# Cross attention blocks with the maximum steps in groups of three and four

## The chip, the cores and the metric

The kernel runs on one core of a Trainium2 chip. The metric is the device time of one execution in microseconds. TensorE does the matmuls and transposes (PE, with its weight loads as PEld), VectorE is DVE, ScalarE is ACT, GpSimd is POOL, and SyncE (SP) issues most DMAs. Each engine takes its own instructions strictly in program order, and semaphores order the engines among each other.

## The reference, cut to what matters

Two post-norm decoder layers on x of shape (4, 1024, 256). Each layer is `x = layernorm(x + self_attention(x))`, `x = layernorm(x + cross_attention(x, ctx))`, `x = layernorm(x + ffn(x))`. The change touches the two cross attentions alone (16 heads of 16, 77 context tokens, a padding mask in the first layer only):

```
Q = x @ Wq + bq ; K = ctx @ Wk + bk ; V = ctx @ Wv + bv     # 16 heads of 16
attn = softmax(Q K^T / 4, over the 77 keys, masked in layer 0)
y = layernorm(x + (attn @ V) @ Wo + bo)
```

## The kernel before, in words

`cross_attention` is called twice, once for each layer (tiles c_...). Its 4096 tokens go in NB = 8 blocks of 512. X, the residual stream, lies in SBUF throughout. One function, `walk`, is run for every engine: it writes down all steps in one order, and each engine takes from each step its own instructions. So the order of the calls in `walk` and `block_of` is the order of work of each engine, POOL's too, and no engine passes a waiting instruction.

The steps of a block n are these.

- `turn_x` (L1006, two halves): PE transposes X, ACT copies it to xT.
- `queries` (L1025, four column groups c): two f32 matmuls, recorded as four; ACT copies to qF with bias and scale; POOL casts to qR.
- `largest` (L1046, sixteen times, c and token tile tt): one matmul of queries with keys into a bank, then a DVE maximum (L1059) that frees the bank.
- `turn_max` (L1064): PE transposes the maxima, ACT copies them to nT, SP writes them by four DMAs into spare rows of qF, so that the later scores come out with the maximum subtracted.
- `scores` (L1084, four times): PE, then ACT's exponential (L1104 with the mask, L1106 without) over psS. There is one psS, so the next scores wait for the exponential.
- `values` (L1109, four times): PE multiplies by V and a column of ones into psO; DVE transposes psO to tok (L1123), takes a reciprocal (L1125), multiplies into oC (L1127), and at every second c transposes oC to oT (L1131).
- `add_bias` (L1138, two halves): POOL makes xb = X + bo.
- `outputs` (L1148, two halves): PE multiplies oT by wo; DVE adds xb to give res (L1166), then computes the moments (bn_stats, bn_aggr, L1169 to L1173); POOL works out the scale and shift in four small operations (rstd, L1182 to L1185).
- `normed` (L1190): ACT writes the normalized rows back to X.

`turn_x`, `queries`, `largest`, `turn_max` and `outputs` share the three PSUM banks of psM in rotation:

```
def bank(w):
    return w.count.get("mi", 0) % RB
```

A step that takes a bank waits until the step three places earlier in that rotation has been read out by DVE or ACT. The blocks are pipelined: during block n the kernel does the maxima of block n+1, the queries of block n+2, and the outputs of block n-1. In the second layer a helper (`hall`, called by `also` and `choice_step`) spreads the token choice of the next stage over blocks 3 to 7: on DVE `weigh` (two operations) and `count` (one operation over 1024 values), on POOL eight indirect DMAs in block 7.

Of the kernel before, what the change touches and what calls it, by code (L numbers as in the profile page):

```python
# [859 lines left out]
def cross_attention(nc, tag, X, y, kv, w_q, b_q, w_k, b_k, w_v, b_v, w_o, b_o, mask, hall=None):  # L860

    B, TK, _ = kv.shape
    NT = X.shape[1]
    H, HD, R, NQ = 16, 16, 32, 4
    BT = 512
    NB = NT * P // BT
# [7 lines left out]
    with ExitStack() as ctx:  # L875
        m = Room(nc, ctx, tag)
# [27 lines left out]
        res = m.sb("res", [P, 2, 2, D])  # L904
# [12 lines left out]
        sems = {n: m.sem(n) for n in names}  # L917
        block = ctx.enter_context(nc.Block())

        came = {}  # L920
# [33 lines left out]
        def keys(w):  # L954
            if w.on("tensor"):
                w.wait("wk", NS)
                for cc in range(2):
                    w.wait(*came["cx", cc])
                for c in range(NQ):
                    for cc in range(2):  # L960
                        last = w.eng.matmul(psS[:, c, 0:B * TK], wk[:, cc, c * P:(c + 1) * P], cxT[:, cc, :],
                                            start=cc == 0, stop=cc == 1)
                    last.then_inc(sems["k"], 1)
            w.inc("k", NQ)
            if w.on("scalar"):
                for c in range(NQ):
                    w.wait("k", c + 1)
                    w.eng.activation(kF[:, c, :], psS[:, c, 0:B * TK], ACT.Identity, bias=bks[:, c:c + 1])\
                        .then_inc(sems["kf"], 1)
            w.inc("kf", NQ)  # L970
            if w.on("vector"):
                for c in range(NQ):
                    w.wait("kf", c + 1)
                    for i in range(4):
                        rows = slice(R * i, R * i + R)
                        kf = kF[rows, c, :].rearrange("p (b k) -> p b k", b=B)
                        if mask is not None:
                            last = w.eng.scalar_tensor_tensor(kblk[rows, c, :, i, :], mbias[rows, :, :], sel17[rows, :], kf,
                                                              ALU.mult, ALU.add)
                        else:  # L980
                            last = w.eng.tensor_copy(kblk[rows, c, :, i, :], kf)
                        last.then_inc(sems["kb"], 1)
            w.inc("kb", 4 * NQ)
# [125 lines left out]
        def values(w, n, c):  # L1109
            b = n // BB  # L1110
            seq = w.count.get("pv", 0)
            if w.on("tensor"):
                if seq < 2:
                    w.wait(*came["v", seq])
                w.wait("ex", seq + 1)
                w.wait("tk", w.at("tk"))
                for i in range(4):
                    last = w.eng.matmul(psO[R * i:R * i + R, :], vP[:, b, 4 * c + i, :], E[:, seq % 2, i, :], start=True, stop=True)
                last.then_inc(sems["pv"], 1)
            w.inc("pv")  # L1120
            if w.on("vector"):
                w.wait("pv", w.at("pv"))
                w.eng.transpose(tok[:, :], psO[:, :]).then_inc(sems["tk"], 1)  # L1123
                w.wait("tk", w.at("tk", -1))
                w.link(w.eng.reciprocal(inv[:, :], tok[:, HD::R]), "dv")  # L1125
                half = c % 2
                w.link(w.eng.tensor_tensor(oC[:, :].rearrange("p (g r) -> p g r", r=R)[:, :, half * HD:(half + 1) * HD],  # L1127
                                           tok[:, :].rearrange("p (g r) -> p g r", r=R)[:, :, 0:HD],
                                           inv[:, :].unsqueeze(2).to_broadcast([P, BT // R, HD]), ALU.mult), "dv")
                if half:  # L1130
                    w.eng.transpose(oT[:, n % 2, c // 2, :], oC[:, :]).then_inc(sems["ot"], 1)  # L1131
            else:
                w.inc("dv", 2)
            w.inc("tk")
            if c % 2:
                w.inc("ot")

        def add_bias(w, n, half):  # L1138
# [9 lines left out]
        def outputs(w, n, half):  # L1148
# [13 lines left out]
            if w.on("vector"):  # L1162
                w.wait("mi", w.at("mi"))
                w.wait("xb", w.at("xb"))
                w.wait("y", w.at("y"))
                w.eng.tensor_tensor(res[:, half, :, :].rearrange("p a c -> p (a c)"), psM[:, k, :],  # L1166
                                    xb[:, half, :, :].rearrange("p a c -> p (a c)"), ALU.add).then_inc(sems[f"m{k}"], 1)
                w.wait(f"m{k}", w.at(f"m{k}", -1))
                w.eng.bn_stats(bst[:, half, 0, :], res[:, half, 0, :])  # L1169
                w.link(w.eng.bn_stats(bst[:, half, 1, :], res[:, half, 1, :]), "dv")  # L1170
                w.eng.memset(idle[:, :], 0.0)
                w.eng.bn_aggr(mv[:, half, 0, :], bst[:, half, 0, :])
                w.eng.bn_aggr(mv[:, half, 1, :], bst[:, half, 1, :]).then_inc(sems["var"], 1)  # L1173
            else:
                w.inc("dv")
            w.inc(f"m{k}")
            w.inc("var")
            if w.on("gpsimd"):
                if n or half:
# [64 lines left out]
        def block_of(w, n):  # L1244

            def big(*cs):
                if n + 1 < NB:
                    for c, tt in cs:  # L1250
                        largest(w, n + 1, c, tt)

            def ask(c):
                if n + 2 < NB:
                    queries(w, n + 2, c)

            def turn(half):
                if n + 2 < NB:
                    turn_x(w, n + 2, half)

            def put(half):
                if n:
                    outputs(w, n - 1, half)

            def norm(half):
                if n:
                    normed(w, n - 1, half)

            def also(c):
                if hall is not None:  # L1270
                    choice_step(w, n, c)

            big((0, 0))
            put(0)
            big((0, 1))
            turn(0)
            big((0, 2))
            scores(w, n, 1)
            big((0, 3))
            turn(1)  # L1280
            big((1, 0), (1, 1))
            also(0)
            values(w, n, 0)
            norm(0)
            ask(0)
            big((1, 2), (1, 3), (2, 0))
            scores(w, n, 2)
            add_bias(w, n, 0)
            big((2, 1), (2, 2))
            ask(1)  # L1290
            also(1)
            values(w, n, 1)
            big((2, 3), (3, 0))
            put(1)
            big((3, 1), (3, 2))
            scores(w, n, 3)
            big((3, 3))
            also(2)
            values(w, n, 2)
            if n + 1 < NB:  # L1300
                turn_max(w, n + 1)
            norm(1)
            add_bias(w, n, 1)
            ask(2)
            ask(3)
            also(3)
            values(w, n, 3)
            if n + 1 < NB:
                scores(w, n + 1, 0)

        def walk(w):
            for cc in range(2):
                turn_context(w, cc)
            keys(w)
            for half in range(2):
                turn_x(w, 0, half)
            for c in range(NQ):
                queries(w, 0, c)
            for half in range(2):
                turn_x(w, 1, half)  # L1320
            if mask is not None:
                turn_mask(w)
            for c in range(NQ):
                for tt in range(4):
                    largest(w, 0, c, tt)
                    if c < 2 and tt == 1:
                        context_values(w, c)
                queries(w, 1, c)
            turn_max(w, 0)
            scores(w, 0, 0)  # L1330
            for n in range(NB):
                block_of(w, n)
            if hall is not None:
                rank(w, 1)
                hall.load(w, 0)
            for half in range(2):
                outputs(w, NB - 1, half)
            for half in range(2):
                normed(w, NB - 1, half)
            if hall is not None:  # L1340
                for t in range(2):
                    hall.scatter(w, 1, t)
# [50 lines left out]
        def _(eng):  # L1393
# [5 lines left out]
            eng.dma_start(wo[:, :, :], w_o.rearrange("(a p) o -> p a o", p=P)).then_inc(sems["wo"], 16)  # L1399
            eng.dma_start(bo[:, :], b_o.partition_broadcast(P)).then_inc(sems["wo"], 16)  # L1400
            eng.preload_act_table(ACT.Exp)
            eng.wait_ge(sems["cstv"], 8)
            walk(Writer(nc, eng, "scalar", sems))

        @block.tensor
        def _(eng):
            eng.wait_ge(sems["cst"], 6)
            eng.wait_ge(sems["cstv"], 8)
            walk(Writer(nc, eng, "tensor", sems))

# [1382 lines left out]
```

## Time and profile before

| | |
|---|---|
| median of 3 runs | 3086.0 us (3080.34 to 3092.77) |
| profiled execution | 3086.83 us, span 3085.1 us |
| granted TensorE clock, mean | 0.94 |
| busy shares of the span | PE 87%, PEld 52%, DVE 55%, ACT 38%, POOL 51% |
| first cross attention | about 1787 to 2059 us of the span |
| second cross attention | about 2646 to 2930 us of the span |

A line of the timeline gives the start, the duration, the engine, the source line, the operation and its tiles, how many instructions were merged, and in brackets how long the engine was idle before it and what released it. Matmuls overlap, so the cost of a step on PE is read from its start to the next step's start.

### The profile page before, as it was taken

The page shows a single profiled execution, that of the slowest core. Times are in us where ns is not written, and L with a number is a line of the kernel's source. Part 1 is how long each engine was busy: PE and PEld are TensorE (multiplying, and loading weights), DVE is VectorE, ACT ScalarE, POOL GpSimd, SP SyncE. Part 2 cuts the span into 40 slices and gives each one's busy share as a digit, 9 for nine tenths or more (in the row PEclk, how much of TensorE's full clock was granted, in tenths as well). Part 3 has the DMA queues.
Part 4 walks back from the last instruction along what each step waited for, and adds up shares of the span by engine and source line. Part 5 has one row for each costly group of instructions (what it writes and reads, how often), then busy time and mean ns, then how long its engine had stood idle before and what let it go on. Part 6 is the DMA issues. An engine that isn't in the chain of part 4 may idle for free. (4 is left out here: it accounts for less than half of the span.)

```text
span 3085.1 us, 40725 instructions
## 1 busy us (share of the span) xinstructions
PE 2689.0 (87%) x11441; PEld 1611.1 (52%) x11441; DVE 1682.7 (55%) x3323; ACT 1176.0 (38%) x1638; POOL 1560.1 (51%) x1298
## 2 busy tenths in 40 slices
PE   7999999999999999999999868971786498588696
PEld 5666666666666666666665433340554244334254
DVE  5665656565565666656566435651223555368753
ACT  3444444444443444444343324540122244244334
POOL 2666667766666776666677712225223312222343
PEclk9999999999999999999999989985998599799798
DMA  4333333323333333333323120024773100000143
GB/s 123 77 78 74 78 80 74 71 70 80 72 80 80 71 72 73 80 70 82 80 70 79 38 85 2 2 69 162 268 266 134 50 1 0 29 2 8 30 136 89
DMA packets 142457, 238.07 MB, mean 77 GB/s; under 512 B 27638, under 2 KB 72990, under 8 KB 137246
## 3 DMA queue, kind: packets, MB, share of 16 engines
q1 hardware_dynamic: 126510, 166.81, 21.7%
q0 software_dynamic: 11904, 64.06, 6.1%
q10 hardware_dynamic: 3952, 6.08, 0.6%
q8 instruction: 47, 0.77, 0.1%
q14 instruction: 44, 0.36, 0.0%
HBM read 89.52 MB, written 29.38 MB: 39 GB/s over the span
## 5 line engine op out<-in xcount | busy, mean ns | idle before, releaser
L636 POOL TENSOR_TENSOR a_total<-a_total,a_pr 128x1024 f32<-128x1024 f32 x384 | 910.6, 2371 | 70.5 <-ACT a_pr L620 50.3
L567 DVE TENSOR_REDUCE a_nmax<-a_psX 128x1 f32<-128x512 f32 x1024 | 694.2, 688 | 150.7 <-PE a_psX L562 148.3
L620 ACT ACTIVATE a_pr<-a_psS 128x1024 f32<-128x1024 f32 x512 | 524.8, 1026 | 656.0 <-PE a_psS L608 650.9
L648 PE MATMUL a_psO<-a_pr,a_vd 128*64 128x512 f32 x2048 | 481.8, 602 | 0.0
L562 PE MATMUL a_psX<-a_kA,a_qA 128*128 128x512 f32 x1024 | 414.7, 406 | 7.7 <-DMA a_kA<-a_klo 4.5
L636 POOL TENSOR_TENSOR a_total<-a_pr 128x1024 f32<-128x1024 f32 x64 | 152.9, 2388 | 516.8 <-ACT a_pr L620 516.8
L608 PE MATMUL a_psS<-a_qA,a_kA 128*128 128x512 f32 x1024 | 347.9, 421 | 1.6 <-DVE a_nT L583 1.4
L608 PE MATMUL a_psS<-a_qB,a_kB 128*128 128x512 f32 x1024 | 322.3, 396 | 1.9 <-DVE a_qB L591 1.9
L648 PEld LDWEIGHTS a_psO<-a_pr,a_vd 128*64 128x64 f32 x2048 | 130.0, 136 | 248.3 <-issue 212.1
L608 PEld LDWEIGHTS a_psS<-a_qA,a_kA 128*128 128x128 f32 x1024 | 184.8, 190 | 124.0 <-issue 90.0
L562 PEld LDWEIGHTS a_psX<-a_kA,a_qA 128*128 128x128 f32 x1024 | 193.8, 189 | 89.9 <-DVE a_nmax L567 15.2
L608 PEld LDWEIGHTS a_psS<-a_qB,a_kB 128*128 128x128 f32 x1024 | 193.6, 189 | 40.6 <-DVE a_qB L591 3.0
L1043 POOL CAST c_qR<-c_qF 128x512 fp32r<-128x512 f32 x64 | 39.2, 613 | 218.4 <-ACT c_qF L1038 218.4
L1059 DVE TENSOR_REDUCE c_nmx<-c_psM 128x4 f32<-128x308 f32 x256 | 110.3, 467 | 64.0 <-PE c_psM L1054 62.6
L582 DVE COPY a_nT<-a_psX 8x128 f32<-8x128 f32 x64 | 17.8, 279 | 222.8 <-PE a_psX L577 222.8
L1033 PE MATMUL c_psM<-c_xT,c_wq 128*128 128x512 f32 x256 | 121.1, 608 | 8.0 <-ACT c_xT L1020 5.3
L1054 PE MATMUL c_psM<-c_kblk,c_qR 128*128 128x308 f32 x256 | 92.8, 404 | 28.3 <-DVE c_nmx L1059 14.3
L480 DVE STREAM_TRANSPOSE a_turned<-a_psM 128x512 f32<-128x512 f32 x64 | 45.9, 717 | 124.7 <-PE a_psM L430 124.7
L2483 ACT ACTIVATE e_hT<-e_psH,e_wt 128x128 f32<-128x128 f32 x160 | 45.6, 368 | 177.8 <-PE e_psH L2475 177.8
L658 ACT ACTIVATE a_oU<-a_psO 128x512 f32<-128x512 f32 x64 | 38.2, 597 | 184.1 <-PE a_psO L648 180.1
L1054 PEld LDWEIGHTS c_psM<-c_kblk,c_qR 128*128 128x128 f32 x256 | 46.3, 192 | 115.3 <-issue 95.6
L2442 PE MATMUL e_psT<-e_ident,e_xg 128*128 128x128 f32 x80 | 19.4, 328 | 93.8 <-DMA e_xg<-sorted_in 93.8
(366 smaller groups left out, 4215.2 us busy)
## 6 DMA issues: line engine op xcount, KB each, us to landing
a_qA<-a_qhi SPq DMA_DIRECT2D x256, 128.0 KB, 2.3
a_kA<-a_khi SPq DMA_DIRECT2D x128, 128.0 KB, 2.3
a_kA<-a_klo SPq DMA_DIRECT2D x128, 128.0 KB, 2.3
a_kB<-a_khi SPq DMA_DIRECT2D x128, 128.0 KB, 2.3
a_qB<-a_qlo SPq DMA_DIRECT2D x128, 128.0 KB, 2.3
a_vd<-a_vg SPq DMA_DIRECT2D x128, 128.0 KB, 2.3
sorted_in<-g_zero SPq DMA_DIRECT2D x4, 1280.0 KB, 11.3
e_xg<-sorted_in SPq DMA_DIRECT2D x40, 128.0 KB, 4.3
```

The source lines that it names most:

```text
L480: w.eng.transpose(turned[:, :], ps[:, :]).then_inc(sems["md"], 1)
L562: w.eng.matmul(psX[:, half, :], qA[:, b, u * P:(u + 1) * P], kA[:, b, half * 512:(half + 1) * 512], start=True, stop=True).then_inc(sems[" ...
L567: w.eng.tensor_reduce(nmax[:, half, u:u + 1], psX[:, half, :], AX.X, ALU.max, negate=True)\
L608: last = w.eng.matmul(psS[:, half, q, :], kt[:, b, kc * P:(kc + 1) * P], qt[:, b, q * 512:(q + 1) * 512], start=a == 0, stop=a == 1)
L620: w.eng.activation(pr[:, n, :], psS[:, half, :, :].rearrange("p a b -> p (a b)"), ACT.Exp, scale=SCALE)\
L636: w.eng.tensor_tensor(total[:, buf, :], first, pr[:, n, :], ALU.add).then_inc(sems["ad"], 1)
L648: last = w.eng.matmul(psO[q * HD:(q + 1) * HD, :], vd[:, b, kc, :], pr[:, n, q * 512:(q + 1) * 512], start=kc == 0, stop=kc == KC - 1)
L1033: last = w.eng.matmul(psM[:, k, :], wq[:, cc, c * P:(c + 1) * P], xT[:, cc, :], start=cc == 0, stop=cc == 1)
L1043: w.eng.tensor_copy(qR[:, n % 2, c, :], qF[:, n % 3, c, :]).then_inc(sems["qr"], 1)
L1054: w.eng.matmul(psM[:, k, 0:K4], qR[:, n % 2, c, tt * P:(tt + 1) * P], kblk[:, c, b, :, :].rearrange("p i k -> p (i k)"), start=True, stop= ...
L1059: w.eng.tensor_reduce(nmx[:, tt, 4 * c:4 * c + 4], psM[:, k, 0:K4].rearrange("p (i k) -> p i k", k=TK), AX.X, ALU.max, negate=True).then_i ...
L2483: last = w.eng.activation(hT[:, par, a, :], psH[:, par, a, :], GELU, bias=wt[:, slot, B1 + a:B1 + a + 1])
```

## The change

The same operations are issued as before, in another order. In `values` the reciprocal, the multiplication and the transpose to oT become a step of their own, `divided`; in `outputs` the moments (DVE) and the scale and shift (POOL) become a step `moments`. `add_bias` is now called right ahead of `outputs` of the same half. The order within a block is rewritten, with the maximum steps in groups of three, three, three, three and four. `turn_x` goes three blocks ahead. In the front of `walk`, two of the four query steps of block 1 stand ahead of the first scores and two behind it, and PE and ACT no longer wait at their start for DVE's constants. Of `block_of` the diff below shows the new order alone; the old one is at L1273 to L1309 above.

```diff
@@ keys
             if w.on("scalar"):
+                w.eng.wait_ge(sems["cstv"], 8)
@@ values
                 w.wait("pv", w.at("pv"))
+                w.wait("dv", w.at("dv"))
                 w.eng.transpose(tok[:, :], psO[:, :]).then_inc(sems["tk"], 1)
-                w.wait("tk", w.at("tk", -1))
+            w.inc("tk")
+
+        def divided(w, n, c):
+            half = c % 2
+            if w.on("vector"):
+                w.wait("tk", w.at("tk"))
                 w.link(w.eng.reciprocal(inv[:, :], tok[:, HD::R]), "dv")
@@ outputs
                                     xb[:, half, :, :].rearrange("p a c -> p (a c)"), ALU.add).then_inc(sems[f"m{k}"], 1)
-                w.wait(f"m{k}", w.at(f"m{k}", -1))
+            w.inc(f"m{k}")
+            came["res", half] = (f"m{k}", w.at(f"m{k}"))
+
+        def moments(w, n, half):
+            if w.on("vector"):
+                w.wait(*came["res", half])
                 w.eng.bn_stats(bst[:, half, 0, :], res[:, half, 0, :])
@@ block_of (the new order; largest is called by big)
             def put(half):
                 if n:
+                    add_bias(w, n - 1, half)
                     outputs(w, n - 1, half)
+
+            def shape(half):
+                if n:
+                    moments(w, n - 1, half)
+            big(3)
+            if n:
+                divided(w, n - 1, 3)
+            ask(0)
+            scores(w, n, 1)
+            big(3)
+            values(w, n, 0)
             put(0)
+            divided(w, n, 0)
+            scores(w, n, 2)
+            big(3)
+            shape(0)
             also(0)
+            values(w, n, 1)
+            put(1)
+            divided(w, n, 1)
             norm(0)
+            big(3)
+            scores(w, n, 3)
+            big(4)
+            shape(1)
+            also(1)
+            values(w, n, 2)
             ask(1)
             if n + 1 < NB:
                 turn_max(w, n + 1)
             norm(1)
+            divided(w, n, 2)
+            also(2)
             ask(2)
             ask(3)
+            if n + 3 < NB:
+                turn_x(w, n + 3, 0)
+                turn_x(w, n + 3, 1)
+            values(w, n, 3)
             also(3)
             if n + 1 < NB:
                 scores(w, n + 1, 0)
@@ walk
+            turn_max(w, 0)
+            for c in range(2):
                 queries(w, 1, c)
-            turn_max(w, 0)
             scores(w, 0, 0)
+            for c in range(2, NQ):
+                queries(w, 1, c)
+            for half in range(2):
+                turn_x(w, 2, half)
             for n in range(NB):
                 block_of(w, n)
+            divided(w, NB - 1, 3)
             for half in range(2):
+                add_bias(w, NB - 1, half)
                 outputs(w, NB - 1, half)
+                moments(w, NB - 1, half)
@@ tensor
-            eng.wait_ge(sems["cst"], 6)
-            eng.wait_ge(sems["cstv"], 8)
+            eng.wait_ge(sems["cst"], 2)
```

## Rows read from the trace of the kernel before

**Rows 1.** Windows: busy PE, PEld, DVE, ACT, POOL; clock, DMA; blocks 1-5 and rest, both attentions.

```profile
1866.87:2005.59 138.72, 123.95 (x624) 56.02 (x621) 86.78 (x210) 70.57 (x75) 37.49 (x71) 1.00 0.01 2
2005.59:2059.40 53.81, 37.75 (x200) 17.36 (x196) 33.72 (x84) 22.51 (x21) 13.27 (x29) 0.90 0.01 1
...
2719.80:2858.60 138.80, 124.59 (x624) 56.12 (x620) 102.78 (x238) 69.17 (x75) 38.17 (x71) 1.00 0.02 6
2858.60:2930.00 71.40, 45.22 (x218) 20.97 (x214) 55.88 (x138) 21.68 (x21) 22.89 (x39) 0.76 0.17 32
```

**Rows 2.** Timeline of PE, first score step of blocks 0, 1 and 7, and of block 0.

```profile
1837.42 2.00 PE L1093 MATMUL c_psS<-c_qF,c_kF 32*77 32x512 f32 x8 [4.41 <-DMA c_qF<-c_nT]
...
1866.87 1.10 PE L1093 MATMUL c_psS<-c_qF,c_kF 32*77 32x512 f32 x8
...
2028.61 2.00 PE L1093 MATMUL c_psS<-c_qF,c_kF 32*77 32x512 f32 x8 [2.63 <-DMA c_qF<-c_nT]
...
2693.80 2.01 PE L1093 MATMUL c_psS<-c_qF,c_kF 32*77 32x512 f32 x8 [4.35 <-DMA c_qF<-c_nT]
```

**Rows 3.** Timeline of PE inside block 2 of the first cross attention.

```profile
1907.28 1.10 PE L1093 MATMUL c_psS<-c_qF,c_kF 32*77 32x512 f32 x8
1908.30 0.55 PE L1054 MATMUL c_psM<-c_kblk,c_qR 128*128 128x308 f32 x2
1908.69 1.88 PE L1033 MATMUL c_psM<-c_xT,c_wq 128*128 128x512 f32 x4
1910.50 1.07 PE L1118 MATMUL c_psO<-c_E,c_vP 77*32 77x512 f32 x8
...
1911.88 1.89 PE L1158 MATMUL c_psM<-c_wo,c_oT 128*128 128x256 f32 x8
```

**Rows 4.** Timeline of ACT and DVE inside blocks 2 and 3.

```profile
1899.14 0.69 DVE L1166 TENSOR_TENSOR c_res<-c_psM,c_xb 128x512 f32<-128x512 f32 x1 [1.72 <-PE c_psM L1158]
...
1900.82 0.83 DVE L1059 TENSOR_REDUCE c_nmx<-c_psM 128x4 f32<-128x308 f32 x2
...
1908.44 1.96 ACT L1104 ACTIVATE c_E<-c_psS,c_mb 77x2048 f32<-77x2048 f32 x1 [1.62 <-PE c_psS L1093]
...
1916.18 1.22 DVE L1059 TENSOR_REDUCE c_nmx<-c_psM 128x4 f32<-128x308 f32 x3
...
1923.33 0.25 DVE L1125 RECIPROCAL c_inv<-c_tok 128x16 f32<-128x16 f32 x1
...
1924.08 0.71 DVE L1131 STREAM_TRANSPOSE c_oT<-c_oC 128x512 f32<-128x512 f32 x1
1924.72 0.44 DVE L1059 TENSOR_REDUCE c_nmx<-c_psM 128x4 f32<-128x308 f32 x1
```

**Rows 5.** Timeline, end of the second layer's self attention.

```profile
2637.58 0.15 DVE L2218 BATCH_NORM_AGGREGATE s_mv<-s_bst 128x2 f32<-128x6 f32 x1
...
2639.35 1.26 POOL L2191 TENSOR_TENSOR s_xb<-X,s_bo 128x512 f32<-128x512 f32 x1
...
2640.71 0.69 DVE L2211 TENSOR_TENSOR s_res<-s_psX,s_xb 128x512 f32<-128x512 f32 x1 [2.98 <-issue]
```

**Rows 6.** PE's wait in block 0, first and second cross attention; windows behind the first.

```profile
1855.96 0.38 PE L1054 MATMUL c_psM<-c_kblk,c_qR 128*128 128x308 f32 x1 [2.55 <-DVE c_nmx L1059]
...
2712.16 0.38 PE L1054 MATMUL c_psM<-c_kblk,c_qR 128*128 128x308 f32 x1 [2.55 <-DVE c_nmx L1059]
...
1858.00:1864.00 6.00, 6.00 (x17) 2.16 (x10) 1.66 (x4) 1.98 (x2) 0.00 (x0) 0.50 0.02 4
```

**Rows 7.** Timeline, front of the first cross attention.

```profile
1795.24 0.32 DVE L1380 TENSOR_SCALAR c_mbias<-c_mraw 128x308 f32<-128x308 uint8 x1 [5.49 <-DMA c_mraw<-mask]
...
1797.88 6.88 PE L961 MATMUL c_psS<-c_cxT,c_wk 128*128 128x308 f32 x16 [0.61 <-ACT c_cxT L936]
...
1815.03 0.87 PE L1054 MATMUL c_psM<-c_kblk,c_qR 128*128 128x308 f32 x2
...
1832.40 0.60 PE L1070 MATMUL c_psM<-c_ident,c_nmx 128*16 128x128 f32 x4
```

More of the change, by code:

```diff
@@ L1122, in values @@
                 w.wait("pv", w.at("pv"))
+                w.wait("dv", w.at("dv"))
                 w.eng.transpose(tok[:, :], psO[:, :]).then_inc(sems["tk"], 1)
-                w.wait("tk", w.at("tk", -1))
+            w.inc("tk")
[3 more added lines that the diff above has]
+                w.wait("tk", w.at("tk"))
                 w.link(w.eng.reciprocal(inv[:, :], tok[:, HD::R]), "dv")
-                half = c % 2
                 w.link(w.eng.tensor_tensor(oC[:, :].rearrange("p (g r) -> p g r", r=R)[:, :, half * HD:(half + 1) * HD],
@@ L1133, in values @@
                 w.inc("dv", 2)
-            w.inc("tk")
-            if c % 2:
+            if half:
                 w.inc("ot")
@@ L1175, in outputs @@
                 w.inc("dv")
-            w.inc(f"m{k}")
             w.inc("var")
@@ L1244, in block_of, with big @@
         def block_of(w, n):
-            def big(*cs):
-                if n + 1 < NB:
-                    for c, tt in cs:
+            steps = [(c, tt) for c in range(NQ) for tt in range(4)]
+            def big(count):
+                for _ in range(count):
+                    c, tt = steps.pop(0)
+                    if n + 1 < NB:
                         largest(w, n + 1, c, tt)
@@ L1255, in ask @@
                     queries(w, n + 2, c)
-            def turn(half):
-                if n + 2 < NB:
-                    turn_x(w, n + 2, half)
             def put(half):
                 if n:
+                    add_bias(w, n - 1, half)
                     outputs(w, n - 1, half)
+            def shape(half):
+                if n:
+                    moments(w, n - 1, half)
             def norm(half):
@@ L1271, in also @@
                     choice_step(w, n, c)
-            big((0, 0))
-            put(0)
[L1275 to L1281, printed above, removed]
+            big(3)
[5 more added lines that the diff above has]
+            values(w, n, 0)
+            put(0)
+            divided(w, n, 0)
+            scores(w, n, 2)
+            big(3)
+            shape(0)
             also(0)
-            values(w, n, 0)
+            values(w, n, 1)
+            put(1)
+            divided(w, n, 1)
             norm(0)
[L1285 to L1289, printed above, removed]
-            ask(1)
[L1291 to L1299, printed above, removed]
+            big(3)
[4 more added lines that the diff above has]
+            values(w, n, 2)
+            ask(1)
             if n + 1 < NB:
@@ L1302, in block_of @@
             norm(1)
-            add_bias(w, n, 1)
+            divided(w, n, 2)
+            also(2)
             ask(2)
             ask(3)
+            if n + 3 < NB:
+                turn_x(w, n + 3, 0)
+                turn_x(w, n + 3, 1)
+            values(w, n, 3)
             also(3)
-            values(w, n, 3)
             if n + 1 < NB:
@@ L1318, in walk @@
                 queries(w, 0, c)
[L1319 to L1322, printed above, removed]
             for c in range(NQ):
@@ L1325, in walk @@
                     largest(w, 0, c, tt)
-                    if c < 2 and tt == 1:
-                        context_values(w, c)
+                    if tt == 1:
+                        if c < 2:
+                            turn_x(w, 1, c)
+                        else:
+                            context_values(w, c - 2)
+                if c == 0 and mask is not None:
+                    turn_mask(w)
+            turn_max(w, 0)
+            for c in range(2):
                 queries(w, 1, c)
-            turn_max(w, 0)
             scores(w, 0, 0)
+            for c in range(2, NQ):
+                queries(w, 1, c)
+            for half in range(2):
+                turn_x(w, 2, half)
             for n in range(NB):
                 block_of(w, n)
+            divided(w, NB - 1, 3)
             if hall is not None:
@@ L1406, in _ @@
         def _(eng):
-            eng.wait_ge(sems["cst"], 6)
-            eng.wait_ge(sems["cstv"], 8)
+            eng.wait_ge(sems["cst"], 2)
             walk(Writer(nc, eng, "tensor", sems))
```

## Prediction

> **What bounds the kernel now.** I read three views: the windows of each cross attention, to see which engine fills them; PE's timeline over one block, to see where PE stands still; and the other engines' timelines, for what releases it. Only the cross attentions are touched, 272 and 284 us of 3085. In blocks 1 to 5 PE is busy 124 of 138.7 us at full clock, DVE 87 (103 in the second attention, which has the token choice), ACT 71 and POOL 37 [rows 1]. So PE's in-order stream sets the pace, with its waits. Five blocks take 138.7 us, 27.74 each. In the second attention blocks 6, 7 and the tail (71.4 us) are another case: PE is busy 45, DVE 56.
>
> **The durations.** PE, start to next start [rows 3]: scores 1.02; two maximum steps 0.39, three about 0.5; queries 1.81 with their tail, 1.72 back to back (estimate from four records); values 1.38 less a pair's 0.39, so 0.99; outputs about 1.7 of the 1.89 recorded. The work of a block is 4 x 1.02 + 16 x 0.15 + 4 x 1.72 + 4 x 0.99 + 2 x 1.7 + about 1.1 of transposes = 21.9 us, which leaves 5.8 us of waits and tails per block to be won. DVE [rows 4]: a maximum 0.41; adding xb 0.70 and the moments 0.98 (together 1.68); reciprocal and multiply 0.75, with the transpose to oT 1.39. Transposing psO to tok takes about 0.75 and starts 1.2 behind values. An exponential starts 1.16 behind its scores and lasts 1.96. DVE starts to add about 2.0 behind the start of outputs, and ACT starts to read a query bank about 1.95 behind its start (estimates: the step's own length plus the lag of 0.3 that scores show).
>
> **The new block, walked.** Let t = 0 be the start of the first scores, with everything at full clock. Maxima 1.0; queries wait for the first bank until 2.0; scores 3.7; maxima 4.8; values 5.3; outputs (first half) 6.3 to 8.0; scores 8.0; maxima 9.0; values 9.5; outputs (second half) 10.5 to 12.2. DVE adds the first half at 8.2, divides to 9.7, does three maxima to 10.9, and the moments end at 12.0. This is where the change bites itself. POOL's order is now: bias of half 0, scale and shift of half 0 (it waits for the moments), bias of half 1. DVE's next addition needs that second bias. What this costs is not shown in the cross attention of before, where both biases are made a half block ahead. But the self attention of the second layer has the same order at its end: the moments end at 2637.73, POOL's bias starts at 2639.35 and DVE's addition at 2640.71, 2.98 us later [rows 5]. So the second addition starts at 15.0 and ends at 15.7. The third maximum behind outputs takes the bank of outputs, so PE stands from 12.5 to 15.8: **one gap of 3.3 us in every block**. Queued behind it are the fourth scores, and on DVE the second division and seven maxima.
>
> From there: scores 15.9; DVE divides to 17.1, then takes seven maxima with four PE steps waiting for three banks, until 19.9; values 19.0; queries 19.9; turn_max 21.7; queries 22.1 and 23.8; two turns of x 25.5; values 26.2; next scores **27.3**. The maxima reach qF in time: in before, turn_max at 1832.40 is followed by the scores at 1837.42 [rows 2, 7], 5.0 us, here 26.7. So the new order, which without POOL's order would make a block of about 24.9 (the second addition at 12.7 in place of 15.0, PE's gap 0.9), makes one of 27.3, 0.4 under 27.74.
>
> **The clock.** The price of the gap is larger than its length. In block 0 of before both attentions have the same wait of 2.55 us [rows 6]. In the first one the clock then fell to 0.50 from 1858 to 1864 and the block took 1866.87 - 1837.42 = 29.45; in the second it held and the block took 2719.80 - 2693.80 = 26.00 [rows 1, 2]. So a fall at this place costs 3.45. After the waits of 2.63, 4.35 and 4.41 the scores ran 2.0 us in place of 1.1: half clock every time [rows 2]. Of five waits of 2.55 and more four ended in the low clock. The new gap is longer than 2.55, and is followed by four sparse maximum steps that wait for DVE, so I expect a fall in nearly every block, lasting until the queries behind it have run a while. Bounds per block: 0 and 3.45. I take 2.7, nearer the upper end: the fourth scores partly hide behind DVE. So 30.0 per block.
>
> The Trainium skill, "TensorE: Matmul & The Clock Gate", section "HAM oscillation — how this bites in real kernels", warns that a recurring wait for an operand sends TensorE back to half rate on each tile anew, not once. It counts only a wait that fills a whole idle period of the gate. Read strictly, that would leave the shorter waits of this kernel free and bring the sum to the case "the clock holds" below; the row of 2.55 us at 1855.96 shows a fall, and the measurement decides.
>
> **The sum.** First and second attention:
>
> - Front. PE no longer waits for DVE's constants ahead of its first transposes, so the keys start when the mask has landed, 1795.2 in place of 1797.9: -2.6 (the second, without a mask, about -2). From the first maximum to turn_max before takes 1832.40 - 1815.03 = 17.4 [rows 7]; with four queries (7) gone behind, and two turns and the mask among the maxima, I walk 12.2. The turns and the mask had stood ahead (-1.5). With the keys at full clock a little earlier turn_max starts at 1822.8. **-9.6**; in the second **-9.0**. The scores still follow 5 us later; two of the four queries fill that wait and keep the clock up.
> - Block 0 gets two queries and two turns more (+4.2), no outputs, fewer waits: I walk 26.1, plus 1.2 for an even chance of a fall: 27.3. Against 29.45 **-2.2**, against 26.0 **+1.3**.
> - Blocks 1 to 5: 5 x 30.0 - 0.7 (no turn in block 5) = 149.3 against 138.7: **+10.6** each. In the second `also(3)` now stands behind the last transpose to tok, and so ahead of the next block's maxima, where nothing covers it: **+2** over three blocks.
> - Block 6, without queries: 1.02 + three groups + the same 3.3 gap gives 25.1 against 23.0 (2028.61 - 2005.59) [rows 1, 2]: **+2.1**; in the second DVE's choice work fills most of it: **+1**.
> - Block 7 and tail, 30.8 before. Outputs of block 6 come behind two scores instead of one; the bias chain of 2.98 comes twice, once in the block and once in the tail, where the second half's addition waits behind the first half's scale and shift. Walked, the last outputs start 5 later and the end is **+7.2**. In the second DVE is busy in this wait anyway: **+4**.
>
> First -9.6 - 2.2 + 10.6 + 2.1 + 7.2 = +8.1, second -9.0 + 1.3 + 12.6 + 1 + 4 = +9.9, together +18 on the profiled 3086.8: 3104.8, and as that run lies 0.8 over the median, **3104**. At no cost I put the split of division and moments into steps (same instructions, waits met), and the added waits of DVE and ACT (old by then).
>
> **Rivals.** What a measurement of this kernel can tell from no change is 0.5%, 15 us.
>
> - *The clock falls as predicted* (3090 to 3120, 3104 the centre): 52 in 100; of these 38 above 3101.4.
> - *The clock holds, or falls in single blocks*: ten blocks at 27.3 give 27 less, 3077. For it speaks the second attention's block 0; against it that the gap is longer. 20 in 100, 17 of it within 0.5%, 3 below.
> - *POOL's chain doesn't bind*, the faster side. Its place is the third maximum behind the second outputs. It decides if the second bias is ready when those outputs end, that is if the first moments end 2.98 earlier, at about 9.5 rather than 12. Then ten blocks at 24.9 give 51 less, and block 7 and the tail some 6 less: 3047. Against it: the additions, the division and three maxima stand ahead of the moments on DVE, 2.7 us from 8.2 on. 15 in 100, all faster.
> - *The low clock outlasts the queries*: the two last queries and the last values run at half speed too, 1.5 to 2 us more per block: 3122 to 3130. 13 in 100, slower.
>
> Faster 18, same 31, slower 51. The range, 3066 to 3124, holds the first two cases and the near edges of the others; the likeliest case alone is 3090 to 3120.
>
> **What would show it.** In the changed trace, POOL's bias of half 1 right behind the four small operations in blocks 1 to 6; DVE's second addition 3 us behind the end of the first moments; a gap of about 3.3 on PE ahead of the third maximum; clock 0.5 for 4 to 8 us behind it, queries at 0.86 us a record; block starts 30 apart (27.3 if the clock holds, 25 if the chain is gone). In the front, turn_max near 1823 and scores near 1828. I would be wrong through the clock (2.7 a block, 27 in all), or through the front (20 in all), walked rather than read.

## The result, and the profile after

The changed kernel takes **3110.8 us** (median of 5 runs, 3109.8 to 3118.2) against 3080.7 (5 runs, 3078.2 to 3092.8): ratio 1.0096, 95% interval 1.0072 to 1.0121. It is slower by about one per cent, and the forecast of 3104 was 7 us short. In the difference it was 12 short: it added 18 to a median of 3086.0, and the kernel before, with two more runs, now has 3080.7. The profiled execution took 3117.9 us, its span is 3116.2.

The windows of both attentions after the change answer to [rows 1]; the cuts are again the first scores of blocks 1 and 6 and the end.

```profile
1853.92:2006.73 152.81, 136.08 (x616) 59.30 (x612) 81.62 (x210) 69.62 (x73) 37.03 (x70) 0.89 0.01 2
2006.73:2071.97 65.24, 43.42 (x200) 18.79 (x196) 31.85 (x84) 22.63 (x21) 15.75 (x31) 0.72 0.00 1
2728.80:2880.75 151.95, 133.69 (x617) 59.07 (x613) 98.12 (x237) 67.82 (x73) 38.64 (x70) 0.90 0.02 5
2880.75:2961.51 80.76, 47.48 (x218) 20.29 (x214) 53.98 (x138) 21.89 (x21) 25.41 (x41) 0.68 0.16 29
```

Five blocks take 152.8 and 152.0 us where they took 138.7 and 138.8. PE's busy time rose from 124 to 136 and 134 with about the same instructions, and the clock is 0.89 where it was 1.00. The rest of the loss is standing still.

The timeline of block 2 of the first attention, which starts at 1884.66, shows both.

```profile
1893.33 0.69 DVE L1171 TENSOR_TENSOR c_res<-c_psM,c_xb 128x512 f32<-128x512 f32 x1 [1.18 <-PE c_psM L1163]
...
1896.81 0.15 DVE L1183 BATCH_NORM_AGGREGATE c_mv<-c_bst 128x2 f32<-128x6 f32 x1
...
1897.10 0.20 POOL L1191 TENSOR_TENSOR c_rstd<-c_mv,c_eps 128x2 f32<-128x2 f32 x1 [5.75 <-DVE c_mv L1183]
...
1897.51 0.64 PE L1055 MATMUL c_psM<-c_kblk,c_qR 128*128 128x308 f32 x2
...
1898.59 1.26 POOL L1149 TENSOR_TENSOR c_xb<-X,c_bo 128x512 f32<-128x512 f32 x1
...
1899.95 0.69 DVE L1171 TENSOR_TENSOR c_res<-c_psM,c_xb 128x512 f32<-128x512 f32 x1 [2.39 <-issue]
...
1900.78 0.38 PE L1055 MATMUL c_psM<-c_kblk,c_qR 128*128 128x308 f32 x1 [2.64 <-DVE c_res L1171]
...
1904.20 1.93 PE L1119 MATMUL c_psO<-c_E,c_vP 77*32 77x512 f32 x8
...
1906.06 3.69 PE L1034 MATMUL c_psM<-c_xT,c_wq 128*128 128x512 f32 x4
...
1915.42 1.10 PE L1094 MATMUL c_psS<-c_qF,c_kF 32*77 32x512 f32 x8
```

The moments of the first half end at 1896.96. POOL's four small operations and the second bias follow, and the addition starts at 1899.95, 2.99 us behind the moments, as in [rows 5]. The trace calls that wait "issue", because it finds no releaser in a semaphore; the row of POOL's bias, which ends 0.1 before, tells who it was. PE's third maximum waits for that addition. It starts 3.27 us behind the start of the pair before it, and for 2.64 of these PE is idle. Then the same values take 1.93 instead of 1.07, and one query 3.69 instead of 1.96. The windows of this stretch show the clock:

```profile
1872.00:1878.00 6.00, 6.00 (x16) 2.25 (x16) 4.29 (x13) 1.43 (x1) 1.29 (x4) 0.50 0.01 3
1904.00:1908.00 4.00, 4.00 (x12) 1.11 (x12) 3.09 (x11) 0.22 (x1) 1.29 (x4) 0.50 0.02 4
1934.00:1940.00 6.00, 6.00 (x15) 2.09 (x15) 3.84 (x12) 0.98 (x1) 1.29 (x4) 0.50 0.01 3
1966.00:1970.00 4.00, 4.00 (x11) 1.18 (x4) 2.60 (x9) 0.00 (x0) 1.29 (x4) 0.50 0.00 0
1996.00:2000.00 4.00, 4.00 (x12) 1.19 (x12) 3.31 (x11) 0.44 (x1) 1.29 (x4) 0.50 0.00 0
```

Those are blocks 1 to 5 of the first attention. Block 6 and the six of the second show it too: 12 of 12 full blocks. The list of waits of the first attention (total us, times, longest) puts the same on one line; in before the wait of the maximum for DVE's addition was 1.5 us in 5 times:

```profile
PE c_psM L1055 <- DVE c_res L1171: 16.2, 6, 3.0
DVE c_res L1171 <- issue: 14.9, 6, 3.0
```

The front and the tail of the first attention:

```profile
1792.40 6.61 PE L961 MATMUL c_psS<-c_cxT,c_wk 128*128 128x308 f32 x16 [2.88 <-DMA c_mraw<-mask]
...
1807.37 0.85 PE L1055 MATMUL c_psM<-c_kblk,c_qR 128*128 128x308 f32 x2
...
1819.42 1.05 PE L1071 MATMUL c_psM<-c_ident,c_nmx 128*16 128x128 f32 x4 [0.57 <-DVE c_vP L1001]
...
1824.75 1.10 PE L1094 MATMUL c_psS<-c_qF,c_kF 32*77 32x512 f32 x8 [0.68 <-DMA c_qF<-c_nT]
...
2065.08 1.26 POOL L1149 TENSOR_TENSOR c_xb<-X,c_bo 128x512 f32<-128x512 f32 x1
2066.43 0.69 DVE L1171 TENSOR_TENSOR c_res<-c_psM,c_xb 128x512 f32<-128x512 f32 x1 [2.98 <-issue]
```

From the first maximum to turn_max it is 12.05 us instead of 17.4 [rows 7]. The wait of 4.41 ahead of the first scores [rows 2] is 0.68, since two queries now lie in it. In the tail the bias chain is there once more, with its 2.98.

Everything is set against each attention's own start (its first load of the context), since the stages outside, unchanged, differ by some us from one profiled execution to another:

| us | turn_max at | block 0 | blocks 1-5 | block 6 | block 7, tail | whole |
|---|---|---|---|---|---|---|
| first, before | 45.2 | 29.5 | 138.7 | 23.0 | 30.8 | 272.2 |
| first, after | 35.0 | 29.2 | 152.8 | 26.9 | 38.3 | 287.6 |
| second, before | 42.8 | 26.0 | 138.8 | 28.2 | 43.2 | 283.9 |
| second, after | 32.6 | 27.4 | 152.0 | 30.2 | 50.6 | 298.0 |

Between turn_max and block 0 lie another 5.0 us before and 5.3 after. The two attentions together are 29.5 us longer, of 31.1 between the spans.

### The profile page after: what moved, and what is told of

It reads as the page before. It is cut to its first block and busy times, and to the rows that moved or that the text cites. A ratio compares the mean times of both kernels' runs of the same rounds, so it can differ in the third digit from the quotient of the medians.

```text
span 3116.2 us, 40775 instructions
## 1 busy us (share of the span) xinstructions
PE 2719.3 (87%) x11441; PEld 1617.7 (52%) x11441; DVE 1664.3 (53%) x3323; ACT 1176.4 (38%) x1638; POOL 1562.6 (50%) x1298
## 5 line engine op out<-in xcount | busy, mean ns | idle before, releaser
L1034 PE MATMUL c_psM<-c_xT,c_wq 128*128 128x512 f32 x256 | 134.7, 667 | 7.0 <-DVE c_nmx L1060 5.1
L1191 POOL TENSOR_TENSOR c_rstd<-c_mv,c_eps 128x2 f32<-128x2 f32 x32 | 6.8, 213 | 216.1 <-DVE c_mv L1183 216.1
L1055 PE MATMUL c_psM<-c_kblk,c_qR 128*128 128x308 f32 x256 | 79.3, 399 | 40.7 <-DVE c_res L1171 33.1
```

Of the source, the lines that this page charges most:

```text
L1034: last = w.eng.matmul(psM[:, k, :], wq[:, cc, c * P:(c + 1) * P], xT[:, cc, :], start=cc == 0, stop=cc == 1)
L1055: w.eng.matmul(psM[:, k, 0:K4], qR[:, n % 2, c, tt * P:(tt + 1) * P], kblk[:, c, b, :, :].rearrange("p i k -> p (i k)"), start=True, stop= ...
```

## The experiments

Seven kernels, in two groups, each timed against the kernel before on the same chip. In the first group (the first four) that one took 3083.1 us (3077.1 to 3089.7), in the second (the last three) 3089.5 (3079.0 to 3097.8). A block's time is from first scores to first scores, and the single blocks quoted are of the first attention unless the second is named.

**1. The chain on POOL taken away.** The changed kernel, with both biases made ahead of the first outputs, in the tail too. There POOL waits for nothing that is new.

```diff
@@ add_bias
-                w.wait("var", w.at("var", 1))
+                w.wait("var", w.at("var"))
@@ block_of, put
-                    add_bias(w, n - 1, half)
+                    if half == 0:
+                        add_bias(w, n - 1, 0)
+                        add_bias(w, n - 1, 1)
                     outputs(w, n - 1, half)
@@ walk, the tail
+            for half in range(2):
+                add_bias(w, NB - 1, half)
             for half in range(2):
-                add_bias(w, NB - 1, half)
                 outputs(w, NB - 1, half)
```

> Both halves' biases are made ahead of the first half's scale and shift, in the blocks and at the tail; nothing else differs from the changed kernel (3110.8). If POOL's order makes the gap of 2.6 to 3.3 us on PE and the gap makes the clock fall, blocks 1 to 5 go from 30.7 to about 25, 57 us in all, and block 6, block 7 and the tail give some 11 more: about 3043. Rival: the gap goes but the sparse maximum steps alone let the clock fall: blocks at 28.3, about 3077. Rival: the chain over POOL is not what binds: 3111.

Measured: 3062.7 us (3058.2 to 3071.4), ratio 0.9937 (0.9922 to 0.9952), so 48 us under the changed kernel and 20 under the one before. Blocks 1 to 4 take 25.9 each, and the clock is 1.00 in every window from 1880 to 1916. The same stretch of block 2 in its timeline:

```profile
1893.47 0.69 DVE L1171 TENSOR_TENSOR c_res<-c_psM,c_xb 128x512 f32<-128x512 f32 x1 [0.34 <-PE c_psM L1163]
...
1894.31 0.38 PE L1055 MATMUL c_psM<-c_kblk,c_qR 128*128 128x308 f32 x1 [0.59 <-DVE c_res L1171]
...
1897.50 1.07 PE L1119 MATMUL c_psO<-c_E,c_vP 77*32 77x512 f32 x8
1898.50 1.98 PE L1034 MATMUL c_psM<-c_xT,c_wq 128*128 128x512 f32 x4
```

The wait of 2.64 is 0.59 and the queries run at full rate. So the order of POOL's work is the cause of both losses; 4.8 of a block's 30.75 us hang on it. What it doesn't yet tell is how the 4.8 divide. The time is 20 above the expected: the block is 25.9 rather than 25, and the clock still fell in block 0 of the first attention (30.8 us) and block 5 of the second (31.6). There PE waits 2.67 us at the same bank (2811.19), but for another reason: DVE does three operations of the token choice ahead of its addition, so this wait isn't POOL's.

**2. The wait kept, the clock kept too.** The changed kernel, with three matmuls into psS ahead of the maximum that waits, in blocks 1 to 6; the wait is as long, PE works in it, and nothing reads what they give.

```diff
@@ block_of, behind the second outputs
-            big(3)
+            big(2)
+            if 0 < n < NB - 1:
+                filler(w, n - 1, 3)
+            big(1)
```

> The changed kernel with three extra f32 matmuls of 512 columns (about 2.6 us, written to the free score bank and read by nobody) ahead of the maximum step that waits, in blocks 1 to 6. The wait for POOL stays as it is. If the fallen clock is worth 3.4 us of a block, blocks go from 30.7 to 27.3 and the kernel, with more work, gets faster: about 3070. Rival: the wait alone is the price and the clock only fills slack: 3111 or a little more.

Measured: 3079.6 us (3074.1 to 3086.5), ratio 0.9991 (0.998 to 1.0001): no different from before. Its timeline at the same place:

```profile
1892.36 0.63 PE L1055 MATMUL c_psM<-c_kblk,c_qR 128*128 128x308 f32 x2
1892.84 2.74 PE L1147 MATMUL c_psS<-c_oT,c_wq 128*128 128x512 f32 x6
1894.82 0.69 DVE L1177 TENSOR_TENSOR c_res<-c_psM,c_xb 128x512 f32<-128x512 f32 x1 [2.40 <-issue]
1895.65 0.38 PE L1055 MATMUL c_psM<-c_kblk,c_qR 128*128 128x308 f32 x1
...
1898.85 1.07 PE L1119 MATMUL c_psO<-c_E,c_vP 77*32 77x512 f32 x8
1899.84 1.98 PE L1034 MATMUL c_psM<-c_xT,c_wq 128*128 128x512 f32 x4
```

The third maximum comes 3.29 behind the pair before it, as in the changed kernel (3.27), and 0.14 behind the end of DVE's addition in both, so it still waits for that and not for the matmuls put in. But the values and queries behind it run at full rate, and blocks 2 to 4 take 27.97 each. That divides the 4.8: the low clock costs **2.8** a block (30.75 - 27.97), the wait alone **2.06** (27.97 - 25.91).

**3. A shorter wait.** The changed kernel, with the first half's moments ahead of the third group of maxima.

```diff
@@ block_of
             scores(w, n, 2)
+            shape(0)
             big(3)
-            shape(0)
```

> The changed kernel with the first half's moments ahead of the third group of maxima, so that POOL's chain starts 1.2 us earlier and PE's gap goes from 3.3 to about 2.1 us. If the clock still falls, each block gains only the 1.2: about 3097. If it holds at 2.1, blocks go to 26.1: about 3056. Rival, the chain doesn't bind: 3111.

Measured: 3077.9 us (3064.0 to 3090.2), ratio 0.9976 (0.996 to 0.9992), between the two expectations. The wait at the bank of outputs is 1.03 to 1.10 in ten of the twelve blocks, and the blocks are of two kinds: 26.7 with the clock at 1.00 and 29.75 (block 2) with it down. In the first attention one block fell. In the second blocks 0, 3 and 5 did (29.1, 31.5, 30.6), but blocks 3 and 5 have longer waits there, 1.83 and 2.78, and block 0 has its wait (1.13) ahead of another maximum. So of the ten short waits one was followed by a fall. One fall costs 3.05 us here (29.75 - 26.7). Its timeline and windows in the block that fell:

```profile
1895.23 0.38 PE L1055 MATMUL c_psM<-c_kblk,c_qR 128*128 128x308 f32 x1 [1.08 <-DVE c_res L1171]
...
1900.51 3.78 PE L1034 MATMUL c_psM<-c_xT,c_wq 128*128 128x512 f32 x4
```

```profile
1892.00:1898.00 6.00, 4.58 (x22) 2.76 (x22) 4.69 (x12) 2.42 (x4) 2.15 (x4) 0.97 0.01 3
1898.00:1904.00 6.00, 6.00 (x14) 1.79 (x14) 3.53 (x11) 0.67 (x1) 1.29 (x4) 0.50 0.00 0
```

**4. The new front alone.** The kernel before with the new order of the front and the shorter waits at PE's and ACT's start; blocks as before.

```diff
@@ walk (turns of x and the mask go among the maxima of block 0)
+            turn_max(w, 0)
+            for c in range(2):
                 queries(w, 1, c)
-            turn_max(w, 0)
             scores(w, 0, 0)
+            for c in range(2, NQ):
+                queries(w, 1, c)
@@ tensor
-            eng.wait_ge(sems["cst"], 6)
-            eng.wait_ge(sems["cstv"], 8)
+            eng.wait_ge(sems["cst"], 2)
```

> The kernel before with the new front alone (queries of block 1 two ahead and two behind the first scores, no wait for DVE's constants at the start), block order as before. The changed kernel's trace has its first scores 9.9 us earlier in each attention. Two queries more in block 0 give back some 3 each if nothing hides them: about 3081 - 14 = 3067. Rival: all of it is given back in block 0: 3081.

Measured: 3067.5 us (3061.6 to 3077.8), ratio 0.9949 (0.9932 to 0.9967), as expected. turn_max comes at 35.6 and 32.6, but block 0 takes 33.0 and 31.3, with the clock at 0.53 from 1842 to 1852: of 9.6 and 10.2 gained, 5.8 and 6.1 are left at the end of the attention. This part alone is a gain; the new blocks turned it into a loss.

**5. The last block in the old order.** Kernel 1, with block 7 in the order of before (the first outputs right behind the first scores, the second behind the second values).

```diff
@@ block_of
+            if n == NB - 1:
+                divided(w, n - 1, 3)
+                put(0)
+                shape(0)
+                scores(w, n, 1)
...
+                divided(w, n, 1)
+                put(1)
+                shape(1)
+                scores(w, n, 3)
...
+                values(w, n, 3)
+                return
             big(3)
```

> The kernel of the first experiment (biases early, 3062.7), with block 7, which has no maxima and no queries, in the order of the kernel before: outputs of block 6 ahead of the second scores. Block 7 and tail are 35.0 and 47.4 us there against 30.8 and 43.2 before. If the late outputs are what costs, that comes back: 3062.7 - 8 = 3054. Rival: the end is set by the two last divisions and outputs in any order: 3062.

Measured: 3063.4 us (3051.6 to 3072.4), ratio 0.9916 (0.9896 to 0.9937). Block 7 and tail are 32.6 against 35.0 in kernel 1 in the first attention, 47.3 against 47.4 in the second: the outputs' place costs 2.5 in the one and 0.1 in the other, where DVE has the token choice to do. That is 2.6 of the 8 us that I expected back. Against kernel 1 the ratios' intervals overlap; it is at best a small gain.

**6. The biases moved, nothing else.** The kernel before, with each bias right ahead of its outputs, as the change has it.

```diff
@@ block_of, put
                 if n:
+                    add_bias(w, n - 1, half)
                     outputs(w, n - 1, half)
...
             scores(w, n, 2)
-            add_bias(w, n, 0)
...
             norm(1)
-            add_bias(w, n, 1)
@@ walk, the tail
             for half in range(2):
+                add_bias(w, NB - 1, half)
                 outputs(w, NB - 1, half)
```

> The kernel before with the bias of each half right ahead of its outputs, as in the changed kernel, and nothing else. In the blocks of before the first half's scale and shift are long done when the second half's bias is due, so blocks stay at 27.7; only the tail has both close together and should get 2.98 per attention: 3083 + 6 = 3089. Rival: moving the bias hurts by itself, each block waits for it: 2 us in 12 blocks, 3107 and more.

Measured: 3102.8 us (3090.7 to 3107.9), ratio 1.0045 (1.0031 to 1.0059). The tail's part is there (2.4 and 3.4 us), and besides it each block takes 28.44 instead of 27.74, which I had put at nothing. Nobody waits for the bias in the old order; it takes DVE's time in another way. POOL's bias and DVE's multiplication of that half in block 2:

```profile
1896.38 1.26 POOL L1144 TENSOR_TENSOR c_xb<-X,c_bo 128x512 f32<-128x512 f32 x1
...
1897.19 0.73 DVE L1127 TENSOR_TENSOR c_oC<-c_tok,c_inv 128x256 f32<-128x256 f32 x1
...
1898.72 1.99 PE L1158 MATMUL c_psM<-c_wo,c_oT 128*128 128x256 f32 x8 [1.35 <-DVE c_oT L1131]
...
1914.29 0.81 DVE L1127 TENSOR_TENSOR c_oC<-c_tok,c_inv 128x256 f32<-128x256 f32 x1
...
1916.36 0.76 PE L1054 MATMUL c_psM<-c_kblk,c_qR 128*128 128x308 f32 x2 [0.96 <-DVE c_nmx L1059]
```

The same two waits of PE in block 2 of the kernel before:

```profile
1897.11 2.00 PE L1158 MATMUL c_psM<-c_wo,c_oT 128*128 128x256 f32 x8 [1.04 <-DVE c_oT L1131]
...
1914.35 0.76 PE L1054 MATMUL c_psM<-c_kblk,c_qR 128*128 128x308 f32 x2 [0.58 <-DVE c_nmx L1059]
```

The multiplication takes 0.73 and 0.81 where it takes 0.42 with POOL idle. The first stands on the way to the outputs, the second ahead of two maxima that free a bank. PE's waits there grow by as much, 1.04 to 1.35 and 0.58 to 0.96, and 0.31 + 0.39 = 0.70 is just what the block lost (28.44 - 27.74). In the changed kernel the biases run beside no multiplication in blocks 1 to 5, and this cost is absent.

**7. Queries in the first block's empty places.** Kernel 5, with two of block 2's queries where block 0 has no outputs.

```diff
@@ block_of, put
+                if not n:
+                    ask(1 + half)
@@ block_of, further down
-            ask(1)
+            if n:
+                ask(1)
...
-            ask(2)
+            if n:
+                ask(2)
```

> As the kernel with the last block in the old order (expected 3054), and in block 0, which has no outputs, the second and third queries stand where the outputs would. In the trace of the first experiment block 0 took 30.8 in the first attention and 27.4 in the second, the former with half clock after the waits ahead of the last four maxima. If the queries keep PE fed there: 4 to 5 less in the first, 1 in the second, about 3049. Rival: the clock falls there anyway and nothing is won: 3054.

Measured: 3059.6 us (3051.1 to 3063.2), ratio 0.9897 (0.9878 to 0.9916), not to be told from kernel 5 (0.9896 to 0.9937); the 3049 isn't reached. In the second attention block 0 is 27.15 instead of 27.4, so the place of those queries costs nearly nothing; in the first the clock was at half around the first scores (1826) and in block 6 (1986 to 1990), so it can't be compared there. It beats the kernel before by 1.0% and the changed one by more, and of the kernels run it has the lowest ratio.

## Why the prediction was right, step by step

- **"One gap of 3.3 us in every block", through POOL's order.** Shown: the third maximum waits in all 12 blocks, the moments-to-addition chain is 2.99 (taken as 2.98), and in kernel 1 the gap goes with the order of two lines on POOL. The length was put somewhat high: PE was to stand from 12.5 to 15.8, and is idle for 2.64 in block 2. The rival "POOL's chain doesn't bind" is out.
- **The clock falls in nearly every block.** 12 of 12 fell. The price was put at 2.7, between 0 and 3.45; kernel 2 gives 2.8, kernel 3 3.05. "The clock holds" (3077) is what kernel 2 makes by force, with 3079.6. "The low clock outlasts the queries" did not come true: the two last queries of block 2, at 1910.02, take 3.60 together, full rate.
- **The block at full clock: mis-sized by 0.67.** Walked 27.3, measured 27.97. Part of it is a step of PE: I had scores follow the first queries after 1.7 and the outputs after 1.7, and the rows of the changed kernel have 1.9 for both (1886.76 to 1888.64, 1891.30 to 1893.22), 0.4 together. The fourth scores stand at 16.43 (walked 15.9), and behind them the walk was right within 0.15 (kernel 2: 11.54, walked 11.4). Without POOL's order the walk gave 24.9 and kernel 1 gives 25.9: the price of the wait itself is 2.06, not 2.4. Five blocks came to +14.1 and +13.2, for +10.6 and +12.6. In the second attention the 2 for the token choice are there (kernel 2: 141.3 against 138.9), while the clock cost less than put, 2.1 a block ((152.0 - 141.3) / 5).
- **The front.** turn_max 10.2 earlier in both, for 9.6 and 9.0.
- **Block 0.** -0.3 and +1.4, for -2.2 and +1.3. With the clock held it takes 27.4 (kernel 5: 27.49; the second attention: 27.39), not 26.1. In the first attention the even chance went the wrong way.
- **Block 6** +3.9 and +2.0, for +2.1 and +1. At full clock it takes 24.6 (kernel 2), under the walked 25.1; the fall of the clock, 2.35 here, was priced in the five blocks and forgotten in this one. In the second attention kernel 2, with the same order and the clock held behind that wait, takes 27.97 there, no more than before (28.15). So the +2.0 is the clock's, and nothing speaks against the reading that DVE's choice work hid the rest.
- **Block 7 and tail** +7.6 and +7.4, for +7.2 and +4. Kernels 1 and 5 divide the first: 3.3 for POOL's chain (38.3 - 35.0), 2.5 for the later outputs, 1.8 left. In the second DVE's choice work was to hide half of it and did not: the chain is 3.2 (50.6 - 47.4), the place of the outputs 0.1, and what the other 4 are stays open.

The terms measured come to +15.4 and +14.1, together 29.5, where the sum had 18. Of the terms only the front came out better than walked. The 11.5 missing are 4.0 in blocks 1 to 5, 2.8 in block 6, 2.0 in block 0, 3.8 in the tails and 0.6 between turn_max and first scores, less 1.7 in the front. So the cause and the size of its main term were right, and the sum was two thirds of what came. That the total lies within 7 us is partly luck: 5 us of the miss are hidden by the lower median of the kernel before.

## What to carry to other kernels

Where an engine works strictly in order, a short operation that is moved "next to its use" may land behind one that waits; look at what now stands ahead of it in its own queue, and make the operand before the chain starts. Give a wait of TensorE its price in clock as well as in length: here 2.06 us of waiting cost 2.8 more in the half clock behind it. And take a bundle apart before judging it: its front alone is 0.5% faster, its blocks with the biases made early take 25.9 us in place of 27.7, and the whole as given is 1% slower.

## What the runs showed of the hardware

**A lock between DVE and POOL.** I had not expected the stretched multiplication. It was already there in before, where it lies off the path (POOL's bias at 1917.90, DVE's multiplication behind it):

```profile
1917.90 1.27 POOL L1144 TENSOR_TENSOR c_xb<-X,c_bo 128x512 f32<-128x512 f32 x1
1918.58 0.87 DVE L1127 TENSOR_TENSOR c_oC<-c_tok,c_inv 128x256 f32<-128x256 f32 x1
```

It isn't a slower rate. Of the 64 multiplications of kernel 6, 40 had neither a bias nor a cast of POOL running when they began, and took 0.42 or 0.43. 24 began beside one, and each ended 0.27 to 0.30 us after POOL's operation, wherever it had started (0.54 to 0.87 long); in before 14 did the same (0.80 to 1.49 long). That is a wait for POOL's end and then the work. The Trainium skill, "SBUF — State Buffer", section "SBUF: two separate sides", says it so: a DVE operation with two inputs in SBUF and a GpSimd one that reads SBUF take an exclusive lock, and the later one blocks. The trace agrees. The token choice has a DVE operation of the same kind, the product of X with a row (0.68 alone): begun beside a bias it took 1.21 in before (2854.74), and 1.54 in kernel 1 (2828.14), and ended 0.55 behind POOL's operation both times. The operations with one input in SBUF or none kept their times beside a bias: the reciprocal took 0.25 at 1896.90 in kernel 6. One row doesn't fit a lock for any operation of POOL: in kernel 1 the multiplication at 1900.07 began beside one of the small operations for the scale (two values a partition, 1899.57 to 1900.26) and took 0.42 all the same.

**The length of a wait does not say whether the clock falls.** All 12 waits at the bank of outputs in the changed kernel, 2.59 to 3.31 us of idle time, were followed by 0.50. But in block 0 of the first attention PE waits 1.14 us ahead of the last maxima in the changed kernel, and the clock falls; in kernel 5 it waits 1.12 at the same place in the same order of work, and the clock holds:

```profile
1842.12 1.53 PE L1055 MATMUL c_psM<-c_kblk,c_qR 128*128 128x308 f32 x4 [1.14 <-DVE c_nmx L1060]
...
1844.57 3.68 PE L1034 MATMUL c_psM<-c_xT,c_wq 128*128 128x512 f32 x4
```

```profile
1839.96 1.54 PE L1055 MATMUL c_psM<-c_kblk,c_qR 128*128 128x308 f32 x4 [1.12 <-DVE c_nmx L1060]
...
1842.42 1.98 PE L1034 MATMUL c_psM<-c_xT,c_wq 128*128 128x512 f32 x4
```

The two block 0 take 29.17 and 27.49 us. Kernel 3 went both ways as well: 1.08 at 1895.23 and a fall, 1.09 at 1925.00 and none. What decides between them isn't shown by any run here. For a forecast this means a chance for each such wait, not a yes or no. It shows from one execution to the next too. Kernel 3's twelve lie 26 us apart, and the mean granted clock falls in step with the time, from 0.940 in the fastest (3064.0) to 0.932 in the slowest (3090.2). Kernel 2, where PE has work in the waits, has twelve within 12 us, with 0.939 to 0.944 in no such order. Which waits fell in the executions without a trace isn't known.
